# Two-layer sequences of a routed two-stage block on one core: statistics taken at once, the input's low half behind the centering, the norm's offset on GpSimd, and the transposes of z between the two halves of the first layer

## What is computed

```python
def layer0(x, c):                      # c: 0 nr, 1 tsr, 2 sr
    two = lambda w1, b1, w2, b2: gelu(x @ w1 + b1) @ w2 + b2
    sr = gelu(gelu(x @ w1_sr + b1_sr) @ w2_sr + b2_sr) @ w3_sr + b3_sr
    y = x + select(c, nr, tsr, sr)     # nr, tsr: two(...)
    return layernorm(y) * gamma + beta
def layer1(x, e):                      # e: one of 16
    h = gelu(x @ down_W.T + down_b)
    h = h @ expert_W[e].T + expert_b[e] + domain_emb[e]
    y = h @ up_W.T + up_b + x
    return layernorm(y) * ln_gamma + ln_beta
```

## Time and profile before

| | before |
|---|---|
| median of 3 runs | 272.14 us (272.11 to 273.24) |
| the profiled execution's own time | 273.42 us |
| its span | 271.6 us |
| PE busy | 254.8 us (94%) |
| PEld busy | 224.6 us (83%) |
| DVE busy | 204.8 us (75%) |
| ACT busy | 193.2 us (71%) |
| POOL busy | 149.5 us (55%) |
| mean granted TensorE clock | 0.98 |

### The profile page before, as it was taken

How to read it: one execution, slowest core, us unless ns; L and a number is a source line. 1 busy time by engine, 2 the same in 40 slices (tenths; PEclk the granted TensorE clock), 3 DMA queues, 4 the chain that set the end, 5 groups by cost and what they waited for, 6 DMA issues and landing times.

```text
span 271.6 us, 8356 instructions
## 1 busy us (share of the span) xinstructions
PE 254.8 (94%) x2118; PEld 224.6 (83%) x2119; DVE 204.8 (75%) x724; ACT 193.2 (71%) x446; POOL 149.5 (55%) x168
## 2 busy tenths in 40 slices
PE   7999999999999998899999999999999999999780
PEld 7798998998998987788888888888888888888460
DVE  6769553474674674898889888888898888888764
ACT  3578479669669666687878888887778888876520
POOL 3134474464674673765655656565655656568352
PEclk9999999999999999999999999999999999999777
DMA  6372011012022122024243423324242433332122
GB/s 181 100 261 64 9 41 42 12 34 58 29 51 72 35 48 69 27 77 97 68 107 85 107 68 87 84 70 101 68 115 77 103 75 80 87 88 68 39 75 80
DMA packets 44098, 20.63 MB, mean 76 GB/s; under 512 B 37782, under 2 KB 42348, under 8 KB 44077
## 3 DMA queue, kind: packets, MB, share of 16 engines
q1 hardware_dynamic: 41385, 15.18, 22.7%
q0 software_dynamic: 1536, 4.20, 4.5%
q10 hardware_dynamic: 1156, 1.00, 1.3%
HBM read 11.69 MB, written 8.65 MB: 75 GB/s over the span
## 4 chain that ended last, share of the span: by engine, by line
PE 58%; SPq 15%; issue 9%; DVE 8%; POOL 3%; ACT 3%; DMA 1%; DVEq 1%; ACTq 1%; POOLq 0%
PE ps_h L1060 15%; PE ps_z L1131 9%; SPq L366 7%; PE ps_u L1183 7%; PE ps_z L1136 4%; PE ps_t L1153 4%; SPq L329 4%; PE ps_z L1095 3%; PE ps_u L1095 3%; SPq L354 3%; PE ps_d L1196 3%; PE ps_t L1234 2%; POOL h_lo L478 2%; PE ps_t L1237 2%; PE ps_t L1235 2%
## 5 line engine op out<-in xcount | busy, mean ns | idle before, releaser
L478 POOL TENSOR_TENSOR h_lo<-h,h_hi 128x256 fp32r<-128x256 f32 (+1 forms) x75 | 70.3, 937 | 75.1 <-ACT h L888 74.3
L485 POOL TENSOR_TENSOR rs<-ve,minus_half 128x4 f32<-128x4 f32 (+1 forms) x38 | 41.2, 1084 | 30.9 <-DVE ve L694 30.7
L895 ACT ACTIVATE zn<-ps_z,nm,rs 128x256 f32<-128x256 f32 x66 | 33.7, 562 | 28.5 <-DVE nm L698 28.5
L888 ACT ACTIVATE h_hi<-ps_h,per_feature_sb 128x256 fp32r<-128x256 f32 x84 | 38.8, 495 | 16.6 <-PE ps_h L1060 14.3
L682 DVE BATCH_NORM_STATS2 st<-ps_z 128x6 f32<-128x256 f32 x66 | 24.9, 418 | 31.9 <-PE ps_z L1136 31.9
L914 ACT ACTIVATE yt<-ps_t,per_feature_sb 128x256 f32<-128x256 f32 x66 | 34.1, 574 | 8.0 <-PE ps_t L1153 8.0
L512 POOL DMA_INDIRECT out<-o,out_rows_now x32 | 34.3, 1071 | 8.0 <-issue 5.4
L888 ACT ACTIVATE h<-ps_h,per_feature_sb 128x256 f32<-128x256 f32 x84 | 38.7, 497 | 0.0
L1131 PE MATMUL ps_z<-last_hi,h_hi 128*128 (+1 forms) x132 | 36.2, 306 | 2.2 <-ACT h_hi L888 0.9
L1183 PE MATMUL ps_u<-tables,stack 65*64 x132 | 36.9, 403 | 0.0
L1183 PE MATMUL ps_u<-second_table,stack 65*64 65x256 f32 x132 | 36.9, 403 | 0.0
(11 more groups left out here) (148 smaller groups left out, 643.1 us busy)
## 6 DMA issues: line engine op xcount, KB each, us to landing
x<-in_x_feat SPq DMA_DIRECT2D x130, 64.0 KB, 2.2
out<-o SPq DMA_DIRECT2D x65, 64.0 KB, 2.1
last_sb<-in_last_w SPq DMA_DIRECT2D x1, 768.0 KB, 4.8
w_sr_sb<-in_w_sr SPq DMA_DIRECT2D x1, 512.0 KB, 3.9
w_sr_sb<-in_w_sr ACTq DMA_DIRECT2D x1, 512.0 KB, 4.8
w_two_sb<-in_w_two SPq DMA_DIRECT2D x1, 512.0 KB, 5.5
out<-o,out_rows_now POOLq DMA_INDIRECT x32, 2.7
per_unit_sb<-in_per_unit SPq DMA_DIRECT2D x1, 268.1 KB
```

What stands on the lines that cost most here:

```text
L478: pool.tensor_tensor(dst, full, high.bitcast(F32), ALU.subtract).then_inc(ready, 1)
L485: pool.tensor_tensor(RS[p][:, norms, :], VE[p][:, norms, :], half_of_two[:, norms, :], ALU.pow).then_inc(rstd, 1)
L888: ins = act.activation(dst[:, m, :], src[m], ACT.Gelu, bias=COL[:, bass.ds(col + m, 1)])
L895: ins = act.activation(ZN[:, t, :], ZP[p][:, t, :], ACT.Identity, bias=NM[p][:, t:t + 1], scale=RS[p][:, 0, t:t + 1])
```

## The change

Five edits, all in the order of work; three small pieces move to another engine.

- VectorE, in all steps but the last ones: the first norm's statistics come ahead of the centering of slot g-3; x_lo follows the centering; then the table copy, now for slot g-1 and not slot g, and the output o, and only then the second norm's statistics and the residual input.
- The offset nm is made by GpSimd, from minus the mean (NEG, a new small VectorE instruction) and rs.
- GpSimd in two-layer steps makes the power and nm ahead of both low halves of h.
- ScalarE in two-layer steps makes x_hi ahead of yt, and zn ahead of the adapter's gelu.
- TensorE in two-layer steps transposes z between the two halves of the first layer, and reads the table addresses (`tables_of`) ahead of the first layer.

```diff
+            def minus_mean(count, p):
+                pool.wait_ge(rstd, count)
+                pool.tensor_tensor(NM[p][:, :], NEG[p][:, :], RS[p][:, 0, :], ALU.mult).then_inc(nmr, 1)
...
                 elif where != HEAD or g >= 0:
                     power(g + 1, p, BOTH)
+                    minus_mean(g + 1, p)
...
                 with pool.Else():
+                    powers(g, i, p, where)
                     for slot in on_slot(g, -1, where):
                         low(h2l[:, 0, :], h2[:, 0, :], h2h[:, 0, :], h0_full, h0_lo, g + 1)
-                    powers(g, i, p, where)
                     for slot in on_slot(g, -1, where):
                         low(h2l[:, 1, :], h2[:, 1, :], h2h[:, 1, :], h1_full, h1_lo, g + 1)
...
             def variances(p, norms):
+                if norms != SECOND:
+                    dve.tensor_scalar(NEG[p][:, :], MV[p][:, 0, :, 0], -1.0, None, ALU.mult)
                 dve.tensor_scalar(VE[p][:, norms, :], MV[p][:, norms, :, 1], EPS, None, ALU.add).then_inc(var, 1)
-            def minus_mean(slot, p, where):
-                dve.wait_ge(rstd, slot + {LAST1: 2, LAST0: 3}.get(where, 1))
-                dve.scalar_tensor_tensor(out=NM[p][:, :], in0=MV[p][:, 0, :, 0], scalar=-1.0, in1=RS[p][:, 0, :],
-                                         op0=ALU.mult, op1=ALU.mult).then_inc(nmr, 1)
...
                 for slot in on_slot(g, 0, where):
                     first_stats(slot, p)
+                    first_moments(slot, p)
+                variances(p, BOTH)
                 for slot in on_slot(g, 3, where):
                     center(slot, q, p)
-                for slot in on_slot(g, 0, where):
-                    first_moments(slot, p)
-                variances(p, BOTH)
                 for slot in on_slot(g, -2, where):
                     input_low(slot, p)
+                for slot in on_slot(g, 1, where):
+                    copy_second_tables(slot, q)
+                for slot in on_slot(g, 3, where):
+                    finish(slot, i - 2 if p == 0 else i - 1, q, where)
...
                         with act.Else():
                             first_of_two(False)
+                            next_input(g, i, p, where)
                             for slot in on_slot(g, 1, where):
                                 residual_norm(slot, q, where)
-                next_input(g, i, p, where)
...
+                    second_of_two()
+                    for slot in on_slot(g, 0, where):
+                        normalise(slot, p, where)
+                    for slot in on_slot(g, 1, where):
+                        adapter_gelu(slot, q)
...
-            def start_two(g, q, where):
+            def start_two(g, q, where, between):
                 weights_ready(where, g + 1, "w1_two")
                 with pe.If(g + 1 < b_nr):
                     pe.wait_ge(x_lo, g + 2)
-                    first_layer_two(q, 0)
+                    first_layer_two(q, 0, 0)
+                    between()
+                    first_layer_two(q, 0, 1)
...
-                start_two(g, 1 - p, where)
-                adapter(g, p, where)
+                at = [tables_of(slot) for slot in on_slot(g, 2, where)]
+                def transposes_of_z():
+                    for slot in on_slot(g, 1, where):
+                        transposes(slot, where)
+                start_two(g, 1 - p, where, transposes_of_z)
+                adapter(g, p, where, at)
```

More of the change, by code:

```diff
@@ L144, in conditioned_layers @@
         RS = [sb(f"rs{p}", [P, 2, TT]) for p in range(2)]
+        NEG = [sb(f"minus_mean{p}", [P, TT]) for p in range(2)]
         NM = [sb(f"nm{p}", [P, TT]) for p in range(2)]
@@ L828, in _ @@
                         second_moments(slot, p, q)
-                for slot in on_slot(g, 0, where):
-                    minus_mean(slot, p, where)
-                for slot in on_slot(g, 3, where):
-                    finish(slot, i - 2 if p == 0 else i - 1, q, where)
                 for slot in on_slot(g, -2, where):
@@ L835, in _ @@
                     add_bias(slot, p)
-                if where == HEAD and g == 0:
-                    dve.wait_ge(s_ct_in, 16)
-                    dve.wait_ge(s_table_act, TABLES_OF_ACT)
-                    dve.wait_ge(s_table_dve, TABLES_OF_DVE)
-                for slot in on_slot(g, 0, where):
-                    copy_second_tables(slot, p)
         @block.scalar
@@ L956, in first_of_two, with second_of_two @@
                         gelu(h2[:, 0:1, :], h2h[:, 0:1, :], [H0[:, 0, :]], first, h0_hi, h0_full)
+                def second_of_two():
+                    for slot in on_slot(g, -1, where):
+                        second = 2 * kind_of(act, slot) + 1
+                        act.wait_ge(h1_ps, g + 2)
+                        gelu(h2[:, 1:2, :], h2h[:, 1:2, :], [H1[:, 0, :]], second, h1_hi, h1_full)
                 with act.If(g + 1 < b_sr):
@@ L1081, in first_layer_sr, with first_layer_two @@
                 ins.then_inc(ready, 1)
-            def first_layer_two(p, row):
-                for m, (bank, ready) in enumerate(((H0, h0_ps), (H1, h1_ps))):
-                    for c in range(KC):
-                        ins = products(bank[:, 0, :], weight("w1_two", row, H, c, m),
-                                       (flat(XH[p][:, c, :, :]), flat(XL[p][:, c, :, :])), c == 0, c == KC - 1)
-                    ins.then_inc(ready, 1)
+            def first_layer_two(p, row, m):
+                bank, ready = ((H0, h0_ps), (H1, h1_ps))[m]
+                for c in range(KC):
+                    ins = products(bank[:, 0, :], weight("w1_two", row, H, c, m),
+                                   (flat(XH[p][:, c, :, :]), flat(XL[p][:, c, :, :])), c == 0, c == KC - 1)
+                ins.then_inc(ready, 1)
             def residual(bank, source):
@@ L1198, in down, with adapter @@
                 ins.then_inc(d_ps, 1)
-            def adapter(g, p, where):
-                at = [tables_of(slot) for slot in on_slot(g, 2, where)]
-                for slot in on_slot(g, 1, where):
-                    transposes(slot, where)
+            def adapter(g, p, where, at):
                 input_residual(g, 1 - p, where)
@@ L1223, in start_two @@
                         pe.wait_ge(x_lo, g + 2)
-                        first_layer_two(q, KC)
+                        first_layer_two(q, KC, 0)
+                    between()
+                    for slot in next_slot(g, q, where):
+                        first_layer_two(q, KC, 1)
             def middle_layer(g, half, highs):
```

32 lines of the change are left out of this document (12 added, 20 removed).

## The result

The changed kernel takes 292.4 us (median of 4 runs, 291.6 to 293.2) where the kernel before took 272.1 beside it: the ratio is 1.0746, with a 95% interval from 1.069 to 1.080. It is slower, as forecast, but by 20.3 us and not by 3.25, and far outside the range of 270 to 279.

The account below looks back on a forecast made before the run. SyncE's queue was taken to set the pace (12.13 us a pair of steps), a ring through the engines having 0.41 us to spare in two pairs; 0.8 + 3.8 + 1.35 - 2.7 = +3.25 gave 275.4 us, range 270.0 to 279.0.

Parts of the forecast that it names:

- The step that failed: VectorE's reordered main loop: earlier statistics, but TensorE isn't waiting for them in two-layer steps, so no effect before the tail.
- GpSimd's order: Power and nm ahead of both low halves: in idle time in a steady two-layer step, so costing nothing there.
- SyncE's ring: Two pairs of two-layer steps, load to freed buffer: 23.85 us rising to 25.21, against the queue's 24.26; +3.8 over four rounds.
- odd loads wait for the residual: Sign expected in the changed profile: odd loads of SyncE's queue wait for the residual, pairs 12.4 to 12.8 us apart.
- the 6.16: TensorE, first layer to next first layer in the step not hanging on the landing: 6.16 us, from 5.96.
- The read: TensorE's 0.54 us read of table addresses, moved between the wait for h_lo and the first layer: +0.56 in each step.
- ScalarE's order: yt behind x_hi in two-layer steps: +0.60 in the step hanging on the landing, +0.20 in the other of a pair.
- nm on GpSimd: The offset made on GpSimd: estimated at 0.3 us, in idle time in a steady step, so costing nothing.
- The tail: At the end, zn no longer waits for VectorE's nm, transposes start about 2.0 us earlier: -2.7, between -0.4 and -3.5.
- The first step and the ramp: First two-layer step +1.2, ramp and three-layer steps -0.4: net +0.8 us at the stretch's first load.
- the sequencer isn't what waits: Rival: the read ahead of TensorE's first layer costs nothing and the pace stays; 270.1 us, faster; chance 0.18.
- The costly nm: Rival: nm on GpSimd costs as much as a power (1.04), each h_lo some 0.5 later; about 281 us; chance 0.08.

Follow-up runs that it names:

- e7: Kernel before with VectorE's new main-loop order alone, nm staying on VectorE: 290.7 us, 1.064.
- e12: Separate test, not this kernel's work: VectorE's operations alone, then each kind beside GpSimd's low halves; copy 283 to 680 ns, statistics 418 beside them.
- e6: Kernel before with GpSimd's power ahead of both low halves, nm staying on VectorE: 278.4 us, 1.016.
- e5: Changed kernel with VectorE's and GpSimd's orders of before, all else as changed: 281.3 us, 1.030.
- e9: Changed kernel with VectorE's order, GpSimd's order and the place of TensorE's read of table addresses as before: 278.8 us, 1.017.
- e11: Kernel before with nm on GpSimd in every step and -mean on VectorE, no order changed: 272.6 us, 0.997.
- e8: Kernel before with nm on GpSimd in the last two steps alone, behind the power: 272.0 us, 0.998.
- e16: Kernel before with VectorE's nm and o alone moved ahead of the second norm's statistics: 318.6 us, 1.165.
- e1: Changed kernel with VectorE's main-loop order of before, -mean on VectorE and nm on GpSimd kept: 288.6 us, 1.053.

## Why the prediction went wrong, point by point

**The step that failed** is the one that read "VectorE does the same work in another order ... nothing comes of it until the tail". The work is the same, its time isn't. In the order before, what ran on VectorE beside a low half was n, the statistics (both read PSUM) and tiny instructions, and h_lo took 0.72 to 0.74 throughout; the new order puts the copies and o there (in e7 the copies and x), and they wait for GpSimd's operation or hold it up (e12). It makes 12.58 us of work in a pair out of 10.6 to 10.7. The trace of before could have warned: of 12.13 us in a pair VectorE was busy for 10.7, gaps of its own take 0.7 more (measured in e7), and so it had some 0.7 us of slack; I looked for what would wait for VectorE, and not at how near it was to its limit. The Trainium skill, SBUF — State Buffer, section Who interferes with whom, has the rule: VectorE and GpSimd share one pair of ports; an operation of VectorE in a two-port mode (which a copy or a tensor_scalar can enter) contends with GpSimd, one with two inputs in SBUF contends with a GpSimd instruction that reads SBUF, and one with at most one input there and outside these modes doesn't. The pairs of operations in e12 agree in all six kinds. I had priced every moved instruction by its duration in its old place.

**GpSimd's order**: the forecast let the power and nm lie "in idle time ahead of the second half's h". Alone the order costs 4.4 us by e6's ratio (2.2 to 6.8), where both low halves now wait for VectorE's statistics; this ring was not in the forecast either.

**SyncE's ring** can't be seen in the changed kernel, where the slower row of VectorE sets the pace. Its small signs are there: yt starts 0.50 behind x_hi (199.46 and 199.96), and in the chain shown the first layer's weight load starts 1.14 behind the end of h_lo. In e5, where both orders are undone, odd loads wait for the residual as the forecast has it:

```profile
SPq L367 <- PE ps_z L1101: 7.8, 10, 1.1
```

But that this wait sets e5's pace is not shown: its chain from 124 to 250 us is TensorE alone, with 6.4 to 6.5 us a step, so TensorE's own row, with its new gaps, is longer than the 6.16 I gave it. The whole ring shows in e9, where the chain of the slow steps runs from SyncE's queue through the landing, x_hi and yt to TensorE. The pairs of e5 are 12.84 us apart up to 172 us and 13.17 behind that, beyond the 12.4 to 12.8 forecast, and e5 costs 8.2 us for 3.25. The terms were mis-sized in both directions. The read was put at 0.56 in each step and shows as 0.16 to 0.27 in the mean: 0.5 to 0.6 where it is not covered, and little or nothing in the other steps; taking it away from e5 gives 3.7 us by the ratios. ScalarE's order was put at 0.60 in one step of a pair and 0.20 in the other, to be paid on the ring alone; taking it back gives 6.0. The forecast had neither the wait for a load ahead of yt nor the power that is held by an earlier x_lo.

**nm on GpSimd** costs nothing in the old order (e11), as forecast, and takes 0.20 us there for the 0.3 estimated; in the changed kernel, where both low halves stand behind it, it takes 0.22 to 0.55, the latter behind an x_lo.

**The tail** was put at -2.7. From the last first layer on the changed kernel gives 1.7, and e8 by itself 0.5, between a gain of 1.4 and a loss of 0.5. The wait for zn is shorter but not gone:

```profile
276.14 0.90 PE L1159 MATMUL ps_t<-ident,zn 128*128 128x128 f32 x4 [0.86 <-ACT zn L897]
277.46 0.63 PE L1101 MATMUL ps_u<-ident,yt 128*128 128x128 f32 x4 [0.43 <-DVE n L724]
```

What stands there next is VectorE's n, the lower end of that term's bounds.

**The first step and the ramp** were put at +0.8, with a gain of 0.4 in the three-layer steps. The first two-layer step loses 0.6 for the 1.2, and the three-layer steps lose 2.1: TensorE waits there 2.5 us for x (60 to 103 us; 0.7 before). With short low halves this is gone, which speaks for the hold again.

**The rivals.** That the sequencer isn't what waits was given 0.18. e9 speaks against it: the read's place matters by 3.7 us. So does the trace of before: from 112 to 242 us TensorE's branch starts 0.06 us behind the end of h_lo in all 21 steps, not in one. The costly nm (281 us) was nearest to the size and wrong in its reason. The right direction came in part by luck: the parts that I had costed do lose (e5), but most of the loss came from one that I had costed at nothing.

Open stays, for the changed kernel and not for e7, how much of what the short low halves give back is the hold and how much the shorter way through GpSimd, and what the transposes between the halves do by themselves, which was not run.

## What to carry to other kernels

Before moving an operation on VectorE, look at what runs on GpSimd in the new place: for a copy, a tensor_scalar or an operation with both inputs in SBUF, add the time that the other engine's operation still has to run to whichever of the two starts second, and keep for such places the operations that read PSUM. An engine for which TensorE doesn't wait can still be 0.7 us away from being the bound: add its own gaps to its busy time and compare with the pace before calling a reordering free. Test parts both ways, one taken back from the changed kernel and one made alone on the old one: here VectorE's order cost 18 us alone, and taking it back gave only 4 to 6, since GpSimd's order held the pace then.

## What the runs showed of the hardware

VectorE and GpSimd don't meet only through semaphores, as the first section has it: operations of certain kinds wait for each other's end. The hold is nearly, not wholly, one after the other. Eight copies and six low halves take 1.70 and 4.13 us apart (the latter beside n), 5.83 in a row, and 4.91 side by side; with o it is 3.25 and 4.13 against 6.10, with x_lo 4.90 and 4.13 against 8.11. It falls on tiny operations as well: nm, two elements a partition, takes 0.69 us in e16 and 0.13 on the same engine where no low half runs. A bias with a fp32 tile of 128x256, 344 ns alone and slower than the 283 of the copy, is held just the same.

Which of the two pays depends on which started first. GpSimd's power of four elements takes 1.38 to 1.58 us where an x_lo of VectorE runs already when it starts, in all 152 such cases of the traces from 40 to 240 us (e12 left out), and 1.01 to 1.04 in the other 359, in most of which an x_lo starts behind it. So it is 1.41 in one step of a pair in e1 and 1.38 to 1.45 in the three-layer steps of before, where x_lo follows the variances, and 1.01 to 1.04 in those of the changed kernel from 56.8 us on, where n stands in between.

With operations handed over one behind the other, the wait can be for several. In e12 GpSimd's first low half comes at 21.15 us, while VectorE works through its row of x_lo; the x_lo go on undisturbed to 23.43, and the low half is through at 24.02, after 2.87 us. Where both rows start together, the two engines take turns, one operation each: a copy takes 0.80 or 0.81 then and a low half 0.77, an x_lo 1.20 and a low half 1.17.
